# Two attention openings of a four-layer kernel: order of the first scores and maxima, and which queue sends which rows of Q

## The reference

```python
def _L0_xattn_ref(q, k, v, Wq, Wk, Wv, Wfc, bfc):      # first layer: 32 heads of 8, keys in 8 groups
    qh = (q @ Wq.T).reshape(N, S_, HEADS, HEAD_DIM).transpose(0, 2, 1, 3)
    ...
    score = jnp.einsum('bhqd,bhkd->bhqk', qh, kh) / math.sqrt(HEAD_DIM)
    attn = jax.nn.softmax(score, axis=-1)
    out = jnp.einsum('bhqk,bhkd->bhqd', attn, vh)
    return out.transpose(0, 2, 1, 3).reshape(N, S_, EMBED) @ Wfc.T + bfc
```

## Time and profile before

| | us |
|---|---|
| median of 3 runs | 1093.73 |
| lowest, highest | 1092.81, 1097.6 |
| the profiled execution | 1096.42 |
| its span in the trace | 1094.7 |

### The profile page before, as it was taken

One profiled execution on the slowest core, in us unless ns is written; L12 is line 12 of the kernel. 1 busy time (PEld: TensorE's weight loads), 2 busy tenths in 40 slices (PEclk: granted clock), 3 DMA queues, 4 the chain that ended last, 5 costly groups with the idle time before them and its releaser, 6 DMA issues. The chain is left out here.

```text
span 1094.7 us, 15369 instructions
## 1 busy us (share of the span) xinstructions
PE 917.0 (84%) x5390; PEld 539.1 (49%) x5416; DVE 616.7 (56%) x1292; ACT 527.1 (48%) x795; POOL 257.8 (24%) x304
## 2 busy tenths in 40 slices
PE   5689897999799548889979665787778799999997
PEld 2334444666469415434436542343345555666664
DVE  4667774444534776715466478999996531211214
ACT  3156664322332574578844237989987212222210
POOL 4001010000000000414433135676776050000014
PEclk9689999899899869989989986555555799999999
DMA  3712410100369102665551636678664021111013
GB/s 111 170 33 52 116 37 11 39 1 1 115 62 67 32 0 78 157 184 128 81 206 26 153 131 128 148 154 187 149 98 78 0 72 49 49 39 48 25 34 101
DMA packets 130828, 91.63 MB, mean 84 GB/s; under 512 B 92997, under 2 KB 120207, under 8 KB 128975
## 3 DMA queue, kind: packets, MB, share of 16 engines
q1 hardware_dynamic: 125906, 83.45, 34.2%
q0 software_dynamic: 1536, 4.20, 1.2%
q10 hardware_dynamic: 3312, 3.02, 0.8%
HBM read 56.09 MB, written 15.86 MB: 66 GB/s over the span
## 5 line engine op out<-in xcount | busy, mean ns | idle before, releaser
L2360 ACT ACTIVATE sb_l_E<-PS,sb_l_NB,sb_L3SQS 128x1024 uint8<-128x1024 f32 x128 | 154.5, 1207 | 25.0 <-DVE sb_l_NB L2413 15.6
L2410 DVE TENSOR_REDUCE sb_l_NM<-PS 128x1 f32<-128x1024 f32 x128 | 155.4, 1214 | 5.4 <-PE PS L2308 5.4
L2308 PE MATMUL PS<-sb_l_K,sb_l_Q 128*128 128x512 bf16 x232 | 116.1, 594 | 47.3 <-ACT sb_l_E L2360 33.1
L2251 POOL CAST sb_l_ET<-sb_l_EP 128x1024 bf16<-128x1024 uint8 x127 | 128.2, 1048 | 62.6 <-DMA sb_l_EP<-sb_l_E 62.6
L613 DVE TENSOR_REDUCE sb_negmax<-PS 128x2 f32<-128x512 f32 x128 | 84.1, 689 | 33.1 <-PE PS L463 32.9
L2318 PEld LDWEIGHTS PS<-sb_L3VI,sb_l_ET 128*128 128x128 bf16 x1024 | 55.2, 112 | 66.1 <-issue 51.0
L599 ACT ACTIVATE sb_E<-PS 128x1024 f32<-128x1024 f32 x64 | 65.5, 1024 | 43.3 <-PE PS L526 43.3
L1368 PE MATMUL PS<-sb_L3w,sb_block_xT 128*128 x184 | 82.8, 593 | 0.7 <-issue 0.7
L923 ACT ACTIVATE sb_E<-PS 128x1024 f32<-128x1024 f32 x64 | 65.3, 1024 | 26.5 <-PE PS L830 22.9
L463 PE MATMUL PS<-sb_K,sb_Q 96*128 96x256 bf16 x256 | 53.8, 302 | 16.1 <-ACT sb_negmax_T L573 10.3
L846 POOL MEMSET sb_rms_eps<- 128x1 f32 x1 | 0.1, 98 | 274.9 <-POOLq L180 274.9
(11 more groups left out here) (357 smaller groups left out, 1731.7 us busy)
## 6 DMA issues: line engine op xcount, KB each, us to landing
sb_Q<-q SPq DMA_DIRECT2D x48, 192.0 KB
sb_L3w<-L3w SPq DMA_DIRECT2D x16, 512.0 KB, 6.9
sb_K<-k SPq DMA_DIRECT2D x24, 192.0 KB
sb_W2E<-L3w SPq DMA_DIRECT2D x8, 512.0 KB, 4.3
q<-sb_q_parts SPq DMA_DIRECT2D x12, 256.0 KB, 4.2
xs<-zero_row SPq DMA_DIRECT2D x1, 2944.0 KB, 47.7
sb_block_x<-xs SPq DMA_DIRECT2D x23, 128.0 KB, 2.2
ys<-sb_block_y ACTq DMA_DIRECT2D x23, 128.0 KB, 2.4
```

Of the source, the lines that this page charges most:

```text
L2251: return eng.tensor_copy(ET[:, u % CRING], EP[:, u // 2 % TRING, :, :, u % 2])
L2308: ins = pe.matmul(core.bank(2 * (n % SRING) + half), Q[:, h % RING, t * P:(t + 1) * P], K[:, h % RING, half * HALF:(half + 1) * HALF], sta ...
L2360: act.activation(E[:, n // 2 % ERING, :, n % 2], S(n), ACT.Exp, bias=NB[:, n:n + 1], scale=scale_of(h, t), accum_out=ZS[:, n:n + 1]).then_ ...
L2410: dve.tensor_reduce(NM[:, n:n + 1], S(n), axis=AX.X, op=ALU.max, negate=True).then_inc(maxed, 1)
```

## The change

In the first attention 12 maxima stand ahead of the steps, the first four steps hold four maxima each (two before and two after the scores), and from step 4 on the order is that of before. turn_max(1) and copy_max(1) move behind step 2. Q of group 0 is sent from SBUF to SBUF in nine transfers. ScalarE issues the rows of maxima itself, behind a wait for its own copy. SyncE loads groups 2 and 3 behind the first and second copy, and later groups behind scored. In the fourth attention ScalarE makes all four copies to QT, SyncE sends both halves of head 0 and then the whole of heads 1 to 3, and VectorE scales Wo at its start. In the diff, a hunk that only takes out_v from a list of semaphores is left out.

```diff
--- before.py
+++ after.py
@@ -338,14 +338,21 @@
 
 
     shared = []
-    for m in range(AHEAD):
+    FIRST = AHEAD - 8
+
+    def maxima_at(s):
+        first, last = (FIRST + 4 * s, FIRST + 4 * s + 4) if s < 4 else (2 * s + AHEAD, 2 * s + AHEAD + 2)
+        return list(range(first, min(last, NM_ALL)))
+
+    for m in range(FIRST):
         shared.append(("max", m))
-        if m in (AHEAD - 9, AHEAD - 1):
-            shared.append(("turn_max", (m + 1 - (AHEAD - 8)) // 8))
+    shared.append(("turn_max", 0))
     after_step = {}
     for s in range(NS):
-        events = [("max", 2 * s + AHEAD), ("max", 2 * s + AHEAD + 1)] if 2 * s + AHEAD < NM_ALL else []
+        events = [("max", m) for m in maxima_at(s)]
         tail_events = []
+        if s == 2:
+            tail_events.append(("turn_max", 1))
         if s % 4 == 3 and (s + 5) // 4 < HALVES:
             tail_events.append(("turn_max", (s + 5) // 4))
         if s % STEPS in (2, 6) and s >= STEPS:
@@ -408,13 +415,8 @@
                         load_k(g, r)
                         load_q(g, r)
 
-                def load_max(n):
-                    g, h = n // 2, n % 2
-                    sp.wait_ge(max_out, n + 1)
-                    for i in range(PARTS):
-                        q = Q[RK + i:RK + i + 1, g % RING, :].rearrange("p (j t) -> p j t", t=TOK)
-                        sp.dma_start(q[:, :, h * HALF:(h + 1) * HALF], MT[PER * i:PER * (i + 1), h, :]
-                                     ).then_inc(m_in[g % RING][h], 16)
+                def send_q(i, r):
+                    sp.dma_start(Q[PR * r + i:PR * (r + 1):PARTS, 0, :], QP[0:R8 * PER, 0, i, :]).then_inc(q_in[0], 16)
 
                 for i, done in enumerate((high, middle, low)):
                     sp.wait_ge(done, 2)
@@ -422,26 +424,27 @@
                 sp.wait_ge(padded, 1 + RING)
                 sp.dma_start(K[RK:RK + PARTS, :, :].rearrange("p r t -> p (r t)"), ones_dram).then_inc(k_ones, 16)
                 for i, done in enumerate((high, middle, low)):
-                    store_q(0, i, done, stored_q0)
                     sp.wait_ge(stored_k[i], 16)
                     load_k(0, i)
-                sp.wait_ge(stored_q0, 16 * PARTS)
-                for r in range(PARTS):
-                    load_q(0, r)
+                    sp.wait_ge(done, 4)
+                    for r in range(PARTS):
+                        send_q(i, r)
+                for i, done in enumerate((high, middle, low)):
+                    store_q(0, i, done, stored_q0)
                 for i, done in enumerate((high, middle, low)):
                     store_q(1, i, done, stored_q1)
+                sp.wait_ge(stored_q0, 16 * PARTS)
                 load(1)
-                load(2)
-                load(3)
+                for g in range(2, RING):
+                    sp.wait_ge(max_out, g - 1)
+                    load(g)
                 sp.wait_ge(stored_q1, 16 * PARTS)
-                for n in range(HALVES):
-                    load_max(n)
-                    g = n // 2
-                    if n % 2 and g >= 1:
-                        if g + RING - 1 < GROUPS:
-                            load(g + RING - 1)
-                        for dst, src in prefetch[g - 1::GROUPS - 1]:
-                            sp.dma_start(dst, src).then_inc(prefetched, 16)
+                for g in range(1, GROUPS):
+                    sp.wait_ge(scored, STEPS * g)
+                    if g + RING - 1 < GROUPS:
+                        load(g + RING - 1)
+                    for dst, src in prefetch[g - 1::GROUPS - 1]:
+                        sp.dma_start(dst, src).then_inc(prefetched, 16)
                 sp.wait_ge(prefetched, 16 * len(prefetch))
 
             @block.tensor
@@ -455,7 +458,7 @@
                 def max_scores(m):
                     g, b, j = m // MAXES, m % MAXES // PER, m % PER
                     if m % MAXES == 0:
-                        pe.wait_ge(q_in[g % RING], 16 * PARTS * (g // RING + 1))
+                        pe.wait_ge(q_in[g % RING], 16 * PARTS * (g // RING + (PARTS if g % RING == 0 else 1)))
                         pe.wait_ge(k_in[g % RING], 16 * PARTS * (g // RING + 1))
                     wait_shared(("max", m))
                     for i in range(2):
@@ -506,14 +509,14 @@
                 ins.then_inc(v_projected, 1)
                 pe.wait_ge(rest, NU)
                 pe.wait_ge(v_out, 1)
-                for kind, i in shared[:AHEAD + 2]:
+                for kind, i in shared[:FIRST + 1]:
                     if kind == "max":
                         max_scores(i)
                     else:
                         turn_max(i)
                 for s, (g, b, kt) in enumerate(steps):
-                    if 2 * s + AHEAD < NM_ALL:
-                        max_scores(2 * s + AHEAD)
+                    for m in maxima_at(s)[:2 if s < 4 else 1]:
+                        max_scores(m)
                     if s == 0:
                         pe.wait_ge(k_ones, 16)
                     if s % 4 == 0:
@@ -527,8 +530,8 @@
                                         K[0:ROWS, g % RING, keys], q[:, 2 * n:2 * n + 2, b * SEQ:(b + 1) * SEQ],
                                         start=True, stop=True)
                     ins.then_inc(scored, 1)
-                    if 2 * s + AHEAD < NM_ALL:
-                        max_scores(2 * s + AHEAD + 1)
+                    for m in maxima_at(s)[2 if s < 4 else 1:]:
+                        max_scores(m)
                     if s >= MIX_LAG:
                         mix(s - MIX_LAG)
                     for kind, i in after_step[s]:
@@ -572,6 +575,11 @@
                         act.wait_ge(m_in[(g - 1) % RING][h], 16 * PARTS * ((g - 1) // RING + 1))
                     act.activation(MT[:, h, :], core.bank_bf16(shared_bank(("turn_max", n)))[0:PARTS * PER, 0:HALF],
                                    ACT.Copy).then_inc(max_out, 1)
+                    act.wait_ge(max_out, n + 1)
+                    for i in range(PARTS):
+                        q = Q[RK + i:RK + i + 1, g % RING, :].rearrange("p (j t) -> p j t", t=TOK)
+                        act.dma_start(q[:, :, h * HALF:(h + 1) * HALF], MT[PER * i:PER * (i + 1), h, :]
+                                      ).then_inc(m_in[g % RING][h], 16)
 
                 def take_sum(s):
                     g, b, kt = steps[s]
@@ -591,7 +599,6 @@
                         act.wait_ge(rest, u + 1)
                         act.activation(part(u, 1), R[0:m, u, :], ACT.Copy).then_inc(middle, 1)
                 copy_max(0)
-                copy_max(1)
                 for s in range(NS):
                     act.wait_ge(scored, s + 1)
                     if s >= ERING:
@@ -601,6 +608,8 @@
                                    ACT.Exp, scale=scale).then_inc(exped, 1)
                     if s > MIX_LAG and (s - MIX_LAG) % 2:
                         take_sum(s - MIX_LAG)
+                    if s == 2:
+                        copy_max(1)
                     if s % 4 == 0 and 2 <= s // 4 + 1 < HALVES:
                         copy_max(s // 4 + 1)
                 take_sum(NS - 1)
...
@@ -2223,12 +2232,12 @@
                 for dst, src in experts[:QUICK]:
                     sp.dma_start(dst, src).then_inc(core.experts_in, 16)
                 sp.wait_ge(out_a, 1)
-                for h in range(RING):
-                    load_q(h, slice(0, HALF), q_in[h])
-                sp.wait_ge(out_a, 2)
-                for h in range(RING):
-                    load_q(h, slice(HALF, TOK), q_late)
-                sp.wait_ge(out_v, 2)
+                load_q(0, slice(0, HALF), q_in[0])
+                sp.wait_ge(out_a, 3)
+                load_q(0, slice(HALF, TOK), q_late)
+                for h in range(1, RING):
+                    load_q(h, slice(0, TOK), q_in[h])
+                sp.wait_ge(out_a, 4)
                 for m in range(NU // 2):
                     sp.wait_ge(exped, 2 * m + 2)
                     if m >= TRING:
@@ -2298,10 +2307,9 @@
                         if t == 0:
                             pe.wait_ge(q_in[h % RING], 16 * (PARTS + 1) * (h // RING + 1))
                         if h == 0 and t == NT // 2:
-                            pe.wait_ge(q_late, 16 * PARTS * RING)
+                            pe.wait_ge(q_late, 16 * PARTS)
                         if n == 2:
-                            pe.wait_ge(out_a, 2)
-                            pe.wait_ge(out_v, 2)
+                            pe.wait_ge(out_a, 4)
                         if n >= SRING:
                             pe.wait_ge(exped, n - SRING + 1)
                         for half in range(2):
@@ -2347,9 +2355,10 @@
             @block.scalar
             def _(act):
                 for half in range(2):
-                    act.wait_ge(q_turned, 2 * half + 1)
-                    act.activation(QT[:, 0, half * HALF:(half + 1) * HALF], core.bank_bf16(4 + 2 * half)[:, 0:HALF],
```

(13 more changed lines are left out.)

4 lines of the change are left out of this document (2 added, 2 removed).

## The result

The changed kernel took 1108.13 us (median; 1104.83 to 1109.44) beside 1094.4 for the kernel before on the same chip: a ratio of 1.0112, interval 1.0079 to 1.0146. The prediction was 1093.3 with a range of 1083 to 1099. The profiled execution took 1107.19 us, with a span of 1105.4, 10.7 longer than before's.

The account below looks back on a forecast made before the run. The prediction took a chain through TensorE to bound the first attention and VectorE the fourth. Opening -5.4, steady cost +11.6 and fourth attention -6.6 summed to -0.4 us, a median of 1093.3 us, range 1083 to 1099.

Parts of the forecast that it names:

- Q of group 0: First attention's opening: sending Q from SBUF to SBUF starts the maxima 2.1 us earlier, bounds 0.7 and 2.3.
- The rows of maxima: First attention's opening: rows issued by ScalarE pass SyncE's backlog; scores start at 48.4 in place of 57.21, bounds 47.9 and 52.
- the forecast of -5.4: First attention's opening up to step 4: all its edits together gain 5.4 us, bounds 1.5 and 7.
- Four maxima per step: First attention, steps 0 to 3: eight maxima moved there give 2.5 us a step; step 4's scores start at 59.4.
- The clock: First attention's opening: 1.2 GHz at first, rising at about 54 us; from there VectorE sets the pace.
- The steady cost: First attention: ScalarE's row issues delay its next exponential and TensorE's mix, 0.73 us a copy; 11.6 us slower, bounds 0 and 24.
- The first rival: Steady part: issues hold ScalarE only in part (1088.4 us) or not at all (1081.7 us); chance 0.17 for each.
- second rival: First attention: ScalarE's issues stretch when SyncE issues a group's loads at the same moment; 1099.6 to 1106 us, chance 0.12.
- The fourth attention: Fourth attention's opening: the wait for Q's late halves goes and Wo's scaling moves earlier; 6.6 us gained, bounds 4 and 7.

## Why the prediction was wrong

**Q of group 0, mis-sized.** 2.1 us was forecast, bounds 0.7 and 2.3. Counted from the first store of K the maxima start 15.12 us on and not 15.69: 0.6, outside the bounds. Of the 1.6 that are missing, 0.7 is the sends (0.70 to 0.73 us each with its gap and not 0.63), 0.3 the last key load (1.02 with its gap and not 0.72), and 0.6 the landing, 2.6 us behind the start of the last send and not 2.0.

**The rows of maxima, the step that failed.** The prediction had the third row issued at 45.9 and landed at 48.4, with "about 0.5 for the loads of groups 1 and 2 in flight". It counted both streams and priced their meeting by a guess. The issues took 2.71 us and the landing came at 51.66; counted from the first maximum the loads cost 2.9 us at the first scores and 4.7 by step 4, as the run without them showed. That run is also the test of all the rest of this term: from the first maximum it took 11.7 us to the first scores and 22.8 to step 4, forecast 11.9 and 22.9, and with the loads beside the rows 14.7 and 27.5. So of the 6.2 us between the forecast of -5.4 and the measured +0.8, Q explains 1.6 and the overlap of rows and loads 4.6. The Trainium skill's rule that each DMA engine alternates between queue rows (DMA: Bandwidth & Descriptors, section Queues, rings and completion order) led me to the low end of my bounds, 47.9 to 52; on the scale of the kernel before, whose first store came 1.08 us later, the scores started at 52.7. I read it so that a row on its own queue passes the backlog; the traces show that it does not pass in time: 3.9 us behind the last issue beside a group's loads, 6.1 behind 1.4 MB of weights, 1.2 alone.

**Why the kernel before was slow there.** The prediction said rightly that the rows stand behind three groups' loads. It did not ask what moving them alone would give. That gave 6.5 us in the opening and 6.4 between the medians (1091.07 and 1097.47), and needed neither ScalarE nor a new order.

**Four maxima per step, wrong sign.** The pace was right (2.5 us a step forecast, 2.6 to 3.0 measured), and so was the remark that the second rows release step 4. Against 20 ahead it loses 2.5 to 2.9 us. I had compared it with the kernel before, in which the late rows hide that. It was tested only with the rows on SyncE.

**The clock, left out.** Step 4's wait of 2.60 us was followed by 1.2 GHz for about 6 us, and the four steps from there took 1.2 us more than the held copy explains. The forecast had the clock rise and stay up. In the run without the loads beside the rows the wait was 0.83 us, and the clock was 1.00 from 56 to 68 us.

**The steady cost, right.** 11.6 us forecast; 0.8 + 10.08 + 2.06 = 12.9 measured. The mechanism held link by link. Most of the difference is the 0.11 us seam behind the third issue, which I had counted as nothing, and 0.58 for an issue where I took 0.573. The first rival, that issues hold ScalarE only in part or not at all, is out where an activation stands behind them; it holds where the issue stands behind the activation. The remark in the Trainium skill (DMA: Bandwidth & Descriptors, section Issuing engines are not separate DMA queues) that the issuing sequencer's time is usually small beside the DMA would have made the term near zero. The trace has 0.58 us for an issue beside 1.2 more to the landing when alone, and three of them in front of a due exponential were the steady loss.

**The stretched issues (second rival, 0.12).** One issue took 1.484 us, but only in the opening, and one took 1.18 with no issue of SyncE beside it; from the fourth copy on the median is 0.580 and the longest 0.678. So the rival's mechanism is out for the steady part. Its time, 1099.6 to 1106, was nearest by luck.

**The fourth attention, right.** 6.6 us forecast; 5.5 from its first turn of Q to its last exponential (195.84 to 190.31) in this profile and 5.9 [3.9 to 7.9] as an edit of its own. Sending the first transposes sooner gave back 0.4 of it, less than I bounded for their lateness.

**Sum.** Forecast -5.4 + 11.6 - 6.6 = -0.4. Measured: opening +0.8 and 1.2 for the clock, steady +12.9, fourth -5.1, end +1.9, start -1.1: 10.6, and 10.7 before rounding. This adds up one pair of profiles. The medians lie 13.7 us apart, and start, end and the layers between vary by some us from profile to profile, so only the terms that a run of its own or a repeated row bears out are shown: the steady cost, the loads beside the rows, the wait for Q that went.

## What to carry to other kernels

Before an issue is moved to a busy engine, look what stands behind it: here it was free directly behind an activation, and in front of one that is due its whole length less the slack was paid. A small transfer that others wait for belongs ahead of the bulk in time; here a queue of its own did not bring it past. And when a wait is found, price the smallest edit that removes it before the large one: the old order with the rows ahead of the loads, together with the fourth attention's edit, has the lowest ratio here (0.985 with Q sent directly, 0.9869 with Q through DRAM), 2.6% below the changed kernel; its interval overlaps that of the next versions.
